# A state-space scan fed by differences of its inputs, in a 12-stage decoder on one core

## The chip, the core and the metric

One core of a Trainium2 chip runs the whole program. The metric is the device time of one launch, in microseconds (us). Engines: PE (TensorE, matmul) with its weight loads (PEld), DVE (VectorE), ACT (ScalarE), POOL (GpSimd), and SP, which here only issues DMAs.

## The reference, cut to the stage that changes

The decoder has four layers of three parts each, and a layer norm closes every part. The change touches one part, the attention slot of layer 2 (L2a in the code), a state-space scan. There are 8 sequences of 256 positions, width 128, with 16 states for each of the 128 channels.

```python
BC = x @ W_in + b_in
Bm, Cm = (BC[..., :N], BC[..., N:])
dt = jax.nn.softplus((x @ W_dt1 + b_dt1) @ W_dt2 + b_dt2)
dt = jnp.clip(dt, 1e-07, 1000000.0)
tmp = A * dt[..., None]
A_bar = jnp.exp(tmp)
B_barX = jnp.expm1(tmp) / tmp * dt[..., None] * Bm[:, :, None, :] * x[..., None]
...
_, h = jax.lax.associative_scan(combine, (A_bar, B_barX), axis=1)
return jnp.sum(h * Cm[:, :, None, :], axis=-1) + D * x
...
x = _layernorm(x + _L2_attn_ref(x, ...), axis=-1)
```

So h[s] = a[s] h[s-1] + (a[s] - 1) / A * B[s] x[s], where a is the decay exp(A dt).

## The kernel before

**Layout.** Channels lie on the partitions. A sequence b is worked off in four chunks t = 4b to 4b+3 of 4 states x 256 positions = 1024 columns, so the stage has 32 chunks. Each engine has its own list of instructions, written out by hand in a loop over t; the constants SCAN_X ... SCAN_DONE say in which iteration the once-per-sequence steps of sequence b come (`due(t, offset, 4)`). An engine works its list strictly in order and waits on semaphores.

**One chunk**, with the lines of the profile:
- ACT, `scan_scaled` (L2474): eight 128x128 products x * B into SBUF (both 128-position halves, four states). `decays` (L2514, L2515): four times exp(A dt) into `decay`, four times tanh(A dt / 2) into `gain`.
- PE, `scan_inputs` (L1809): eight transposes bring x * B, channels on partitions, into two PSUM banks (0 and 1, or 2 and 3).
- DVE, `feed` (L3375): (decay + 1) * PSUM. POOL, `scan_gains` (L855): that times tanh, which makes (a - 1) B x; it also clears the first decay of each state (L854).
- DVE, `scan` (L3383): the recurrence over the 1024 columns, both operands from SBUF. Then (L3387) the states times C, which PE has spread over the partitions in banks 4 and 5 (`spread_c`, L1895: four fp32 matmuls with a 16-row operand).
- PE, `summed` (L1911): eight matmuls with diagonal matrices 1/A add the states into bank 6; L1906 adds D * x.

In the trace each of these fp32 matmuls is two rows (it is worked in two halves), and a transpose is one row.

**Once per sequence**, all of it in bank 7: transpose of x (`scan_turn_x`, L1784; copied by ACT L2434), projections C and low rank (`scan_project`, L1789, L1790; ACT L2444, L2445), step size and B (`scan_step_sizes`, L1795, L1797; DVE `scan_sized` L3264, L3267), softplus as a series (ACT L2452, L2454, L2461; DVE `scan_series` L3274, L3277 and `scan_softplus` L3298, L3299), and at the end residual (L3392), statistics (L3398, L3401), root on POOL (L864, L865) and norm (L3407).

**Before and behind.** The gated part L1f runs ahead of the stage and already holds the first steps of sequences 0 and 1; the attention part L2x follows.

## Time and profile before

| | |
|---|---|
| median of 3 runs | 1743.04 us (1739.76 to 1743.62) |
| span of the profiled execution | 1740.7 us |
| scan stage, first scan to the last norm | 765.1 to 974.9 us |
| one sequence in the middle of the stage | 26.7 us |
| ACT busy in that sequence | 25.57 us |
| DVE busy in that sequence | 25.57 us |
| PE busy in that sequence, clock 1.00 | 22.72 us |

The profiled execution is known by its span, 1740.7 us; the median of the runs lies 2.3 us above it. Busy times are unions of an engine's rows, and those of PE hold the modelled tail of a matmul too. A clock of 1.00 is 2.4 GHz, 0.50 is 1.2 GHz.

### The profile page before, as it was taken

How to read it: one execution, taken by the hardware profiler on the slowest of the kernel's cores; microseconds unless marked ns; L12 is line 12 of the kernel's file. 1: busy time of each engine (PE TensorE's matmuls, PEld its weight loads, DVE VectorE, ACT ScalarE, POOL GpSimd, SP SyncE). 2: the span in 40 equal slices, each digit the busy share in tenths (PEclk: the TensorE clock that was granted, in tenths of full speed). 3: DMA queues.
4: the chain of work that ended last, by engine and by line, in shares of the span. 5: the costliest groups of instructions: out<-in, count | busy, mean ns of one | idle time of the engine just before them, and what ended most of it. 6: DMA issues, size and time to landing. Idle time of an engine off the chain costs nothing.

```text
span 1740.7 us, 34480 instructions
## 1 busy us (share of the span) xinstructions
PE 1516.1 (87%) x12731; PEld 1088.4 (63%) x12741; DVE 1273.2 (73%) x2817; ACT 1069.6 (61%) x2219; POOL 691.6 (40%) x801
## 2 busy tenths in 40 slices
PE   6588868799998898889989999998989998989875
PEld 5344436578777555667768766665548994655542
DVE  2688863697775798479999667758873448858988
ACT  4499942367665577399999155546763443157765
POOL 2455635578887022356767313320000101511223
PEclk9799979899999999989898989999998999999985
DMA  3200121200000000010000100000000000000000
GB/s 133 111 13 14 37 93 37 61 10 2 1 1 1 2 2 2 4 37 1 1 1 1 58 2 2 2 13 1 2 2 1 1 1 11 1 19 2 2 2 25
DMA packets 14791, 30.94 MB, mean 18 GB/s; under 512 B 1537, under 2 KB 10145, under 8 KB 13857
## 3 DMA queue, kind: packets, MB, share of 16 engines
q1 hardware_dynamic: 13602, 26.63, 4.4%
q0 software_dynamic: 1024, 2.10, 0.4%
q8 instruction: 104, 1.70, 0.4%
q14 instruction: 61, 0.50, 0.1%
HBM read 22.42 MB, written 6.29 MB: 16 GB/s over the span
## 4 chain that ended last, share of the span: by engine, by line
PE 44%; DVE 15%; ACT 14%; issue 12%; POOL 12%; DMA 1%; SPq 0%; POOLq 0%; DVEq 0%; ACTq 0%
PE PS L1412 5%; PE PS L1472 4%; ACT big L2261 4%; POOL big L837 4%; DVE negmax L2802 3%; PE PS L1744 3%; PE PS L1733 3%; POOL big L825 3%; ACT big L2239 2%; PE PS L1494 2%; POOL big L833 2%; PE PS L1417 2%; PE PS L1911 2%; PE PS L1895 2%; DVE V L3383 2%
## 5 line engine op out<-in xcount | busy, mean ns | idle before, releaser
L2239 ACT ACTIVATE big<-PS 128x1024 f32<-128x1024 f32 (+1 forms) x256 | 249.0, 974 | 163.4 <-PE PS L1423 162.7
L2802 DVE TENSOR_REDUCE negmax<-PS 128x4 f32<-128x1024 f32 x192 | 235.0, 1224 | 54.3 <-PE PS L1412 52.2
L1412 PE MATMUL PS<-KS,QS 32*128 32x256 f32 (+1 forms) x1152 | 133.2, 316 | 36.1 <-DVE negmax L2802 25.9
L1412 PEld LDWEIGHTS PS<-KS,QS 32*128 32x128 f32 x1152 | 86.7, 187 | 109.7 <-DVE negmax L2802 71.5
L711 POOL TENSOR_TENSOR rstd<-veps,mhalf 128x2 f32<-128x2 f32 x72 | 51.3, 712 | 242.2 <-DVE veps L2676 232.7
L1423 PE MATMUL PS<-QS,KS 32*128 32x256 f32 (+1 forms) x1152 | 133.7, 319 | 1.4 <-ACT big L2239 1.4
L1472 PE MATMUL PS<-big,V 128*32 128x256 f32 (+1 forms) x2048 | 133.0, 378 | 0.4 <-ACT big L2239 0.4
L737 POOL TENSOR_TENSOR res<-resb,XB 128x256 f32<-128x256 f32 x24 | 17.4, 727 | 258.5 <-ACT resb L2325 258.5
L779 POOL TENSOR_SCALAR KT<-QT 128x1024 f32<-128x1024 f32 x64 | 66.6, 1040 | 66.6 <-DVE QT L2821 62.7
L2821 DVE SCALAR_TENSOR_TENSOR QT<-PS,wint 128x1024 f32<-128x1024 f32 x64 | 77.3, 1220 | 17.9 <-PE PS L1365 17.2
L1423 PEld LDWEIGHTS PS<-QS,KS 32*128 32x128 f32 x1152 | 84.8, 188 | 5.8 <-issue 4.0
L2416 ACT ACTIVATE QT<-PS,W 128x256 f32<-128x256 f32 x128 | 53.6, 470 | 55.6 <-PE PS L1733 55.6
L825 POOL TENSOR_SCALAR big<-big,rsum 128x256 f32<-128x256 f32 (+1 forms) x144 | 60.7, 434 | 68.0 <-DVE rsum L2723 67.6
L1468 PE MATMUL PS<-big,V 128*32 128x512 f32 x512 | 64.5, 623 | 23.0 <-ACT big L2261 17.0
L837 POOL TENSOR_TENSOR big<-big 128x512 f32<-128x512 f32 x64 | 81.3, 1270 | 5.0
L1472 PEld LDWEIGHTS PS<-big,V 128*32 128x32 f32 x2048 | 54.1, 110 | 43.7 <-issue 14.3
L1129 PE MATMUL PS<-OT,W 128*128 128x256 f32 x272 | 75.5, 400 | 6.4 <-ACT QT L2187 6.4
L2187 ACT COPY QT<-PS 64x256 f32<-64x256 f32 x128 | 46.8, 366 | 53.0 <-DVE big L2707 51.3
L2261 ACT ACTIVATE big<-KT,W 128x1024 f32<-128x1024 f32 x64 | 73.0, 1141 | 9.0 <-POOL KT L779 9.0
L1895 PE MATMUL PS<-OT,SEL 16*128 16x256 f32 x256 | 67.5, 405 | 11.9 <-DVE V L3387 10.8
L1911 PE MATMUL PS<-On,V 128*128 128x128 f32 x512 | 77.2, 315 | 0.0
L1911 PEld LDWEIGHTS PS<-On,V 128*128 128x128 f32 x512 | 71.9, 225 | 7.9 <-issue 7.9
(479 smaller groups left out, 4323.8 us busy)
## 6 DMA issues: line engine op xcount, KB each, us to landing
W<-in_wpack SPq DMA_DIRECT2D x1, 4180.0 KB, 13.9
W<-in_wpack SPq DMA_DIRECT2D x1, 2560.0 KB, 9.0
W<-in_wpack SPq DMA_DIRECT2D x1, 2449.5 KB, 8.0
y_rows<-one_more SPq DMA_DIRECT2D x1, 2048.0 KB, 9.0
masks<-in_mask SPq DMA_DIRECT2D x8, 256.0 KB, 2.9
x_rows<-x_tok SPq DMA_DIRECT2D x16, 128.0 KB, 2.1
W<-in_wpack SPq DMA_DIRECT2D x1, 1538.0 KB, 5.9
x_tok<-in_x SPq DMA_DIRECT2D x1, 1024.0 KB, 4.8
```

Of the source, the lines that this page charges most:

```text
L825: ins = nc.gpsimd.tensor_scalar(PRW[:, u % 4, c0:c1], PRW[:, u % 4, c0:c1], rsum[:, u % 16, j:j + 1], 1.0, ALU.mult, ALU.mult)
L837: nc.gpsimd.tensor_tensor(q, q, RTW[:, u % 4, :, :], ALU.add).then_inc(sem("t_rope"), 1)
L1129: mm = nc.tensor.matmul(PS[:, QKB[u % 2], k * S:(k + 1) * S], w(f"{n}_w{x}", h * P, (h + 1) * P), OT[:, b, :], start=True, stop=True)
L1412: mm = nc.tensor.matmul(PS[:, MAXB[half], o], QS[r, bm % 2, tm, j * P:(j + 1) * P], KS[r, bm % 2, tm, k], start=not a.causal, stop=last)
L1423: mm = nc.tensor.matmul(PS[:, exp_banks(ge)[half], o], KS[r, be % 2, te, kb * P:(kb + 1) * P], QS[r, be % 2, te, q], start=not a.causal, s ...
L1472: mm = nc.tensor.matmul(out_rows[:, skip:S], v, PX[:, T % 2, h, kb * S:(kb + 1) * S - skip], start=first, stop=last)
L1895: mm = nc.tensor.matmul(PS[:, CB + k // 2, (k % 2) * S:(k % 2 + 1) * S], SEL[:, 4 * c + k, :], C_rows(b), start=True, stop=True)
L1911: mm = nc.tensor.matmul(PS[:, YB, j * P:(j + 1) * P], chunk("h", t)[:, at:at + P], by_state[:, 4 * c + k, :], start=False, stop=c == 3 and ...
L2239: nc.scalar.activation(PX[:, T % 2, 2 * p:2 * p + 2, 0:cols], PS[:, exp_banks(g)[0]:exp_banks(g)[0] + 2, 0:cols], ACT.Exp, scale=a.scale). ...
L2261: nc.scalar.activation((PX, PX2)[k][:, T % 2, 2 * p:2 * p + 2, :], clipped((QT, KT)[k], g), ACT.Exp, scale=a.scale, bias=w(("high_base", " ...
L2802: ins = nc.vector.tensor_reduce(negmax[:, h:h + 2, :].rearrange("p h j -> p (h j)"), banks.rearrange("p h (j k) -> p (h j) k", j=2), AX.X, ...
L2821: nc.vector.scalar_tensor_tensor(clipped(QT, g), PS[:, pair_banks(g):pair_banks(g) + 2, :], -100.0 / a.scale, capT[:, g // PAIRS % 2, :].u ...
```

## The change

The scan is summed by parts. Write v[s] = B[s] x[s] and leave the 1/A to the diagonal matrices, so that h[s] = a[s] h[s-1] + (a[s] - 1) v[s]. With g[s] = h[s] + v[s+1] this becomes g[s] = a[s] g[s-1] + (v[s+1] - v[s]): the scan's input is a difference of neighbours, and a - 1 is not needed. At the end x[s+1] times the sum over states of C[s] B[s+1] / A is taken off ("crossed"). In detail:
- ACT: `decays` makes only the exponentials (the tanh row is gone), in 255 columns each, since the first decays stay zero. `scan_scaled` makes four products instead of eight; POOL makes the other half in one instruction of 512 columns. New on ACT: `start` (copies the 4 first states into the PSUM chunk, once per chunk), the first decay and first inputs, one more projection copy, and `copy_result`. Two DVE jobs (bias and absolute value of the step size) go to ACT.
- PE: `scan_inputs` no longer transposes. It multiplies by a matrix of differences `L2a_ahead`, eight fp32 matmuls of 128 columns, and twice per chunk a matmul of 2 columns bridges the halves. `spread_c` uses the reduced fp32 type F32R on a 48-row operand that holds C as two parts. `summed` has the states as the moving operand, four matmuls of 256 columns. New per sequence: a projection of B, the matmul for the first inputs, `cross`, and `result`, two transposes back.
- DVE: `feed` is gone; the scan takes its second operand from PSUM. New per sequence: `scan_crossed_rows` (two instructions on 16 partitions), `crossed_inputs`, and `read_y` in place of the residual.
- POOL: `scan_gains` is gone; new are `scan_scaled`, `scan_signed`, `scan_first_state`.

```diff
-SCAN_X, ..., SCAN_DT, SCAN_Y, SCAN_DONE = -9, -8, -7, -6, -5, -4, -3, 5, 7
+SCAN_X, ..., SCAN_DT = -9, -8, -7, -6, -5, -4, -3
+SCAN_START, SCAN_CROSS, SCAN_Y, SCAN_OUT, SCAN_STATS, SCAN_DONE = -2, 2, 4, 6, 7, 8
...
-            def scan_gains(t):
-                pool.wait_ge(sem("L2a_fed"), t + 1)
...
-                nc.gpsimd.tensor_tensor(chunk("gain", t), chunk("gain", t), fed_to(t), ALU.mult).then_inc(sem("L2a_gain"), 1)
+            def scan_scaled(t):
...
+                if t >= 2:
+                    pool.wait_ge(sem("L2a_xB"), t - 1)
+                nc.gpsimd.tensor_tensor(chunk("x", t)[:, 512:1024].rearrange("p (k d) -> p k d", k=4),
...
+            def scan_first_state(b):
+                pool.wait_ge(sem("L2a_bc"), 2 * b + 3)
+                pool.wait_ge(sem("L2a_decay"), 5 * b + 1)
...
             def scan_inputs(t):
                 pe.wait_ge(sem("L2a_xs"), t + 1)
+                pe.wait_ge(sem("L2a_xs_second"), t + 1)
                 if t >= 2:
-                    pe.wait_ge(sem("L2a_fed"), t - 1)
-                for k in range(4):
-                    for j in range(2):
...
-                        mm = nc.tensor.transpose(PS[:, bank, (k % 2) * S + j * P:(k % 2) * S + (j + 1) * P],
-                                                 chunk("x", t)[:, at:at + P], ident)
+                    pe.wait_ge(sem("L2a_scan"), t - 1)
+                b, c = t // 4, t % 4
+                for h in range(2):
...
+                        nc.tensor.matmul(bank[:, first:first + P], chunk("x", t)[:, k * P:(k + 1) * P], w("L2a_ahead", 1),
+                                         start=k % 2 == 0, stop=False)
+                    nc.tensor.matmul(bank.rearrange("p (k c) -> p k c", k=2)[:, :, P - 1], x_tok[0:1, 2 * b + 1, :],
+                                     B_cols(b)[0:1, 16 + 4 * c + 2 * h:18 + 4 * c + 2 * h], start=False, stop=False)
...
+                def cross(b):
+                    bank_free(b)
+                    nc.tensor.matmul(PS[:, 7, 0:S], w(f"{n}_AT", rows=16), CB_rows(b), start=True, stop=True)\
...
+                def result(b):
+                    pe.wait_ge(sem(f"{n}_y_read"), 2 * b + 2)
...
                 for t in range(4 * B + 1):
-                    if t >= 4 and t + 2 < 4 * B:
-                        scan_inputs(t + 2)
+                    if 0 < t < 4 * B:
+                        spread_c(t)
+                    if t:
+                        summed(t - 1)
                     if (b := due(t, SCAN_PROJECT, 4)) is not None:
...
+                    if t + 2 < 4 * B:
+                        scan_inputs(t + 2)
+                result(B - 1)
...
                     for k in range(4):
-                        i, at = 4 * c + k, slice(k * S, (k + 1) * S)
-                        nc.scalar.activation(chunk("decay", t)[:, at], step_size(b), ACT.Exp, scale=w(f"{n}_A", i, i + 1))
-                        ins = nc.scalar.activation(chunk("gain", t)[:, at], step_size(b), ACT.Tanh, scale=negmax[:, i, 0:1])
+                        i = 4 * c + k
+                        ins = nc.scalar.activation(chunk("decay", t)[:, k * S + 1:(k + 1) * S], step_size(b)[:, 1:S], ACT.Exp,
+                                                   scale=w(f"{n}_A", i, i + 1))
...
+                def start(t):
+                    act.wait_ge(sem(f"{n}_xB"), t + 1)
...
+            def scan_crossed_rows(b):
+                dve.wait_ge(sem("L2a_bc"), 2 * b + 2)
...
-                def feed(t):
...
-                    dve.wait_ge(sem(f"{n}_gain"), t + 1)
+                    dve.wait_ge(sem(f"{n}_decay"), t + t // 4 + 2)
+                    dve.wait_ge(sem(f"{n}_started"), t + 1)
...
-                    nc.vector.tensor_tensor_scan(h, chunk("decay", t), chunk("gain", t), 0.0, ALU.mult, ALU.add)\
+                    nc.vector.tensor_tensor_scan(h, chunk("decay", t), flat(PS[:, bank:bank + 2, :]), 0.0, ALU.mult, ALU.add)\
```

The order of PE's instructions, from the matmuls with C of one chunk on. On PE before, one iteration with the projections and the next (OT holds C, On the diagonals, W and QT the transposes):

```order
L1895 MATMUL PS<-OT,SEL 128x256 x4
L1911 MATMUL PS<-On,V 128x128 x8
L1809 MATMUL PS<-W,QT 128x128 x8
L1789 MATMUL PS<-KT,W 16x256
L1790 MATMUL PS<-KT,W 64x256
L1895 MATMUL PS<-OT,SEL 128x256 x4
```

The same place of PE in the changed kernel, whose own line numbers these are (L1987 is the spread of C, L1999 the sum, L1895, L1897 and L1901 the differences of one half chunk, L1868 to L1870 the projections):

```order
L1987 MATMUL PS<-KS,SEL 128x256 x4
L1999 MATMUL PS<-V,On 128x256 x4
L1868 MATMUL PS<-KT,W 16x256
L1869 MATMUL PS<-KT,W 64x256
L1870 MATMUL PS<-KT,W 16x256
L1895 MATMUL PS<-W,QT 128x128 x2
L1897 MATMUL PS<-rt,x_tok 128x2
L1901 MATMUL PS<-W,QT 128x128 x2
L1895 MATMUL PS<-W,QT 128x128 x2
L1897 MATMUL PS<-rt,x_tok 128x2
L1901 MATMUL PS<-W,QT 128x128 x2
L1987 MATMUL PS<-KS,SEL 128x256 x4
```

The eight transposes have become ten matmuls, and they moved from ahead of the projections to the very end of the iteration, right in front of the next spread of C.

On DVE before, from the product with C of the chunk in which a step size falls due to the next one:

```order
L3387 TENSOR_TENSOR V<-V,PS 128x1024
L3277 SCALAR_TENSOR_TENSOR xs<-masks,xs 128x256 x2
L3392 TENSOR_TENSOR res<-PS,x_tok 128x256
L3298 SCALAR_TENSOR_TENSOR OT<-OT,xs 128x256
L3299 SCALAR_TENSOR_TENSOR KT<-OT,KT 128x256
L3375 SCALAR_TENSOR_TENSOR one_more<-big,PS 128x1024
L3383 SCALAR_TENSOR_TENSOR V<-big 128x1024
L3387 TENSOR_TENSOR V<-V,PS 128x1024
```

The same place of DVE in the changed kernel (L3542 is the product with C, L3554 `read_y`, L3412 and L3413 the crossed rows, L3433 the series, L3457 and L3458 the softplus, L3538 the scan):

```order
L3542 TENSOR_TENSOR V<-V,PS 128x1024
L3554 TENSOR_TENSOR XB<-PS,XB 128x256
L3412 TENSOR_TENSOR KS<-one_more,KS 16x256
L3413 SCALAR_TENSOR_TENSOR one_more<-PS,W,one_more 16x255
L3433 SCALAR_TENSOR_TENSOR xs<-masks,xs 128x256 x2
L3457 SCALAR_TENSOR_TENSOR OT<-OT,xs 128x256
L3458 SCALAR_TENSOR_TENSOR KT<-OT,KT 128x256
L3538 SCALAR_TENSOR_TENSOR V<-big,PS 128x1024
L3542 TENSOR_TENSOR V<-V,PS 128x1024
```

The 1024-column feed ahead of the scan is gone, and two 16-partition rows that wait for this sequence's projections stand between `read_y` and the series.

## Rows read from the trace of the kernel before

**Rows 1.** The page: span, busy time of each engine.
```profile
span 1740.7 us, 34480 instructions
PE 1516.1 (87%) x12731; PEld 1088.4 (63%) x12741; DVE 1273.2 (73%) x2817; ACT 1069.6 (61%) x2219; POOL 691.6 (40%) x801
```
**Rows 2.** Windows: start:end, length, busy us (rows) per engine, clock, DMA.
```profile
core 0: us, PE busy (x) PEld busy (x) DVE busy (x) ACT busy (x) POOL busy (x), PEclk, DMA share, GB/s
785.00:944.30 159.30, 146.46 (x861) 120.82 (x861) 151.85 (x165) 153.75 (x440) 108.91 (x61) 0.91 0.00 1
865.40:892.10 26.70, 22.72 (x145) 18.22 (x144) 25.57 (x28) 25.57 (x74) 18.09 (x10) 1.00 0.00 1
785.00:799.00 14.00, 14.00 (x89) 11.29 (x89) 12.97 (x12) 14.00 (x41) 9.41 (x5) 1.00 0.00 1
800.00:803.00 3.00, 3.00 (x15) 3.00 (x15) 3.00 (x3) 3.00 (x10) 1.70 (x2) 0.50 0.03 5
```
**Rows 3.** Groups of ACT by line, 865.4 to 892.1 us.
```profile
L2474 ACT ACTIVATE QT<-x_tok,rt 128x128 f32<-128x128 f32 x32 | 9.7, 386 | 0.0
L2515 ACT ACTIVATE big<-KT,negmax 128x256 f32<-128x256 f32 x16 | 7.9, 494 | 0.0
```
**Rows 4.** Groups of DVE by line, 865.4 to 892.1 us.
```profile
L3383 DVE TENSOR_TENSOR_SCAN V<-big 128x1024 f32<-128x1024 f32 x4 | 9.1, 2284 | 0.0
L3387 DVE TENSOR_TENSOR V<-V,PS 128x1024 f32<-128x1024 f32 x4 | 4.9, 1221 | 0.1
L3375 DVE SCALAR_TENSOR_TENSOR one_more<-big,PS 128x1024 f32<-128x1024 f32 x2 | 2.4, 1216 | 0.8 <-ACT big L2515 0.8
L3274 DVE SCALAR_TENSOR_TENSOR xs<-KT 128x256 f32<-128x256 f32 x1 | 1.3, 1283 | 0.0
L3267 DVE TENSOR_SCALAR OT<-PS,W 128x256 f32<-128x256 f32 x1 | 0.5, 474 | 0.0
```
**Rows 5.** Chain that ended last, pieces: start us, us to the next piece.
```profile
825.25 0.55 PE PS L1797 x4
834.27 1.92 PE PS L1895 x8
836.19 1.98 PE PS L1911 x16
838.17 0.87 PE PS L1809 x8
839.04 0.22 PE PS L1784 x2
844.03 0.54 PE PS L1789 x2
```
**Rows 6.** POOL's 512-column product elsewhere: ns min/median/max.
```profile
L837 POOL TENSOR_TENSOR big<-big x64: 1261/1269/1323, 333.9 to 551.2; 128x512 f32<-128x512 f32 x64
```
**Rows 7.** Timeline where the stage starts: start, us, idle before in brackets.
```profile
764.73 2.59 POOL L855 TENSOR_TENSOR big<-big,wint 128x1024 f32<-128x1024 f32 x1
765.14 4.33 DVE L3383 TENSOR_TENSOR_SCAN V<-big 128x1024 f32<-128x1024 f32 x1
770.77 1.35 PEld L1895 LDWEIGHTS PS<-OT,SEL 16*128 16x128 f32 x4 [3.49 <-DVE V L3387]
```
**Rows 8.** Timeline of DVE: products with C of chunks 3, 27 and 31.
```profile
789.28 1.22 DVE L3387 TENSOR_TENSOR V<-V,PS 128x1024 f32<-128x1024 f32 x1
...
948.43 1.22 DVE L3387 TENSOR_TENSOR V<-V,PS 128x1024 f32<-128x1024 f32 x1
...
968.01 1.22 DVE L3387 TENSOR_TENSOR V<-V,PS 128x1024 f32<-128x1024 f32 x1
```
**Rows 9.** Timeline where the stage ends.
```profile
971.85 0.69 PE L1264 MATMUL PS<-misc,W 32*128 32x256 f32 x2
971.96 0.42 DVE L3392 TENSOR_TENSOR res<-PS,x_tok 128x256 f32<-128x256 f32 x1 [2.72 <-PE PS L1911]
974.28 0.62 DVE L3407 SCALAR_TENSOR_TENSOR x_tok<-res,mv,rstd 128x128 f32<-128x128 f32 x2 [1.09 <-POOL rstd L865]
```

More of the change, by code:

```diff
@@ L27 @@
 CAPACITY = 256
-CONSTS, EARLY = 12, 6
+CONSTS, EARLY = 13, 6
 TERM = 8
@@ L521, in z_of, with first_inputs, first_decay, first_state @@
             return OT[:, 6 + b % 2, :]
-        low_rank, series = OT[0:64, 4, :], xs[:, :, :].rearrange("p j c -> p (j c)")
+        low_rank, series = OT[64:128, 4, :], xs[:, :, :].rearrange("p j c -> p (j c)")
+        crossed, summed_x = (XB[:, k, :, :].rearrange("p j d -> p (j d)") for k in range(2))
+        scan_zeros = big[:, 0:4096].rearrange("p (n c) -> p n c", c=S)[:, :, 0:1]
+        signed_B = sums[0:2, :, :].rearrange("p a b -> p (a b)")
+        def first_inputs(b):
+            return KT[:, 7, 136 + 32 * (b % 2):168 + 32 * (b % 2)]
+        def first_decay(b):
+            return KT[:, 7, 200:216]
+        def first_state(b):
+            return KT[:, 7, 216 + 16 * (b % 2):232 + 16 * (b % 2)]
+        def result_bank(b):
+            return 4 if b == B - 1 else 7
         def u_of(b):
@@ L2538, in L2a @@
                         decays(t + 2)
+                    if t + 1 < 4 * B:
+                        start(t + 1)
+                    if t == -1:
+                        scan_turned_x(2)
+                    elif t % 4 == 3 and 3 <= (t + 9) // 4 <= B:
+                        scan_turned_x((t + 9) // 4)
+                    if (b := due(t, SCAN_PROJECT, 4)) is not None:
+                        scan_projected(b)
+                    if (b := due(t, SCAN_STEP_SIZE, 4)) is not None:
+                        scan_small_exponential(b)
+                    if (b := due(t, SCAN_OUT, 4)) is not None:
+                        copy_result(b)
+                    if (b := due(t, SCAN_RATIO, 4)) is not None and b >= 2:
+                        scan_squares(b, 2)
+                    if (b := due(t, SCAN_U, 4)) is not None:
+                        scan_squares(b, 0)
             def L3a():
@@ L3429, in L2a @@
                         scan_series(b, 3, 5)
-                    if (b := due(t, SCAN_Y, 4)) is not None:
+                    if (b := due(t, SCAN_STATS, 4)) is not None and b < B - 1:
                         deviations(b)
+                deviations(B - 1)
+                norm(B - 1)
             def L3a():
```

305 lines of the change are left out of this document (204 added, 101 removed).

## The prediction

> **What bounds the kernel now.** I read the page first: in the whole program PE is busy 87% and DVE 73% [rows 1], an average over twelve stages that says little of one. The change lives in 210 us of it, so the windows of this stage come next. In one sequence in its middle, 26.7 us long, ACT and DVE are each busy 25.57 us and PE 22.72 us, at a clock of 1.00 [rows 2]. So two engines share the bound and PE has 4 us to spare. Over six sequences (785.0 to 944.3) it looks the same, with one difference: the mean clock of PE is 0.91 [rows 2]. A clock is 1.00 or 0.50, so PE spent 18% of 159.3 us, about 29 us, at half clock, and lost 14 us of work there, 2.4 us a sequence. That was free as long as ACT and DVE set the pace.
>
> The products with C give the rhythm: chunk 3 at 789.28, chunk 27 at 948.43, chunk 31 at 968.01 [rows 8]. Six sequences in 159.15 us make 26.5 us each. The start is worse than the middle: the first scan took 4.33 us, where the mean of later ones is 2.28, since POOL's L855 had started just before it; PE then stood idle for 3.49 us behind it [rows 4, 7].
>
> **The change, part by part, per sequence (four chunks).**
>
> ACT: sixteen tanh rows go. Sixteen rows cost 7.9 us, and as many exponentials stay. Of 32 scaling products (9.7 us) half go, 4.85 us [rows 3]. Added: four `start` copies, first decay, first inputs, one projection copy, two step-size rows in place of one, `copy_result`. The trace has no row of 4 or 16 columns on ACT; bounds are nothing and the 386 ns of a 128-column product [rows 3]. I take 0.35 us each, since small rows do not get much shorter, for nine rows 3.2 us. ACT: 25.57 - 7.9 - 4.85 + 3.2 = 16.0 us. It is no bound any more, even at 386 ns each.
>
> DVE: four feeds go, each 1.21 us, 4.8 in all, and the bias row of 0.47 [rows 4]. Added: two rows on 16 partitions and `crossed_inputs`, three rows like the 0.42 us of L3392 [rows 9], plus the step between two, 1.35 us. `read_y` replaces L3392 at its price. That gives 21.6 us. The scan now reads PSUM. That form is not in the trace; it lies between no change (the product L3387, also SBUF with PSUM, costs 1.22 us for 1024 columns, the feed of the same kind 1.22) and the 4.33 us of the slow first scan [rows 4, 7]. I take 2.3, by the two rows with a PSUM operand. POOL has less to do: its one 1024-column product (2.59 us and more [rows 7]) becomes a 512-column one, 1.27 us [rows 6]. DVE rows that stretch beside POOL now, such as the 1.28 us of L3274 at a width where L3392 takes 0.42, can shorten, by up to 2.5 us a sequence. So 19.1 to 21.6 us, and with two waits that the new order puts on DVE (the crossed rows stand behind ACT's three projection copies; the norm stands right behind the statistics and POOL's root, which took 1.09 us of waiting at the end [rows 9]) about 22.5.
>
> PE, from the pieces of the chain at full clock [rows 5]:
> - Spread of C: 8 rows of 0.24 us become 4 rows of one pass. A row of 128 columns of an fp32 matmul, which is half the matmul's work on half the columns, takes 0.124 (1.98 / 16); 256 columns in one pass I take at 0.12, at most 0.24. 4 x (0.48 - 1.92) = -5.8 us, at the dear end -3.8.
> - Differences in place of transposes: 8 rows, 0.87 us, become 16 rows of 0.124, 1.98 us: 4 x 1.11 = +4.4 us.
> - Two bridging matmuls of 2 columns per chunk are 4 rows; L1797 with 16 columns takes 0.55 / 4 = 0.137 each: +2.2 us. Below, 0.11 as for a transpose: +1.7.
> - Once: B's projection and `cross`, each like L1789, 0.54; the first inputs 0.27; `result` like L1784, 0.22: +1.6 us.
>
> Together +2.4 us (+4.4 with the dear spread). By pieces PE's work of before is 4 x (1.92 + 1.98 + 0.87) = 19.1 and some 3.0 for the rest, 22.1 us; the 22.72 busy hold tails of matmuls whose next one waited. After: 24.5 us. PE becomes the bound, against 26.5 for a sequence now.
>
> Does anything add to PE's own work? I walked one sequence with these durations. PE's iteration is spread, sum, extras, differences. The differences of chunk t+2 need the end of scan t (they overwrite its bank). The scan starts when the previous product with C is through, the product starts some 0.6 us after the iteration, and PE reaches the differences 2.4 us into it at the earliest, 4.1 with the projections. That fits in three iterations of four. In the one after the projections it is close: ACT copies them from about 4.1 us on, DVE does the crossed rows until 6.4, series and softplus until 8.2, the next scan until 10.5, while PE wants that scan's end at 10.6. One DVE row of the series that stands behind POOL's 1.27 us product costs PE up to 1.2 us. I add half of that, 0.6: 25.1 us a sequence. Queued behind PE's wait are the next spread and with it DVE's product, so what is lost there is lost for the stage.
>
> **PE's clock** decides whether 25.1 holds. The half-clock stretches of before lie in the stage's spread rows and waits (800 to 803: 15 rows in 3 us, clock 0.50, ahead of it 785 to 799 with no idle time and clock 1.00 [rows 2]). In the changed kernel the 16-row spread, 40% of PE's time in a chunk, shrinks to a tenth, full-height matmuls fill the rest, and the waits that PE has now (3.49 us at the start [rows 7]) mostly go. I take the clock as full in the middle of the stage. The trace also speaks against it, since 785 to 799 was dense and a fall came all the same. The Trainium skill (TensorE: Matmul & The Clock Gate, "What's actually happening") says that activity releases the throttle; by that alone a PE that never waits would stay at full clock, and the sum would be the one without falls. Rows 2 disagree with it in this form, so the falls keep a chance below.
>
> **The sum.**
> - Middle: 6 x (25.1 - 26.5) = -8.4 us.
> - Start: the first scan no longer waits behind feed and series (about 2 us), does not meet L855 (4.33 - 2.28 = 2.05 us), and PE does not wait 3.49 us for it and then work at half clock. These overlap; by the same walk chunk 3's product comes at 781 to 784 in place of 789.28: -5 to -8, taken as -6. The Trainium skill (SBUF — State Buffer, "Who interferes with whom") says that a DVE instruction with one SBUF input does not contend with GpSimd and one with two does; the 4.33 us row agrees, and it would give the 2.05 us in full.
> - End: from the last product (968.01) to the norm (974.28) come two transposes, an ACT copy and their handoffs, +1.3 us; L2x's first matmul (971.85 [rows 9]) stands behind them on PE, +1.2. The four last chunks, 19.6 us now, have no differences to make and stay as they are within 1 us.
> - Ahead, L1f: one 1024-column clear and half products on POOL, hidden in DVE's and POOL's waits there; nothing, at worst +1.
>
> -8.4 - 6 + 1.3 = -13.1 us against the profiled 1740.7, that is 1727.6; the median stands 2.3 above the span, so 1730 us.
>
> **Rivals.**
> - All handoffs hide and small rows are cheap: PE 24.0, start -8: 6 x -2.5 - 8 + 1.3 = -21.7, 1721 us. For it: ACT and POOL have much slack. Against it: the tight place above. Chance 0.17.
> - The half clock stays as it was: 2.4 us a sequence now fall on the bounding engine: 27.5 us. +6 - 4 + 1.3 = +3, 1740 to 1746 us. For it: falls in dense stretches. Against it: the spread of 16 rows shrinks. Chance 0.15, split over all three signs.
> - DVE's order becomes the bound (crossed rows waiting for ACT, the norm for POOL's root, series rows behind POOL): 26.3 us a sequence, -1.2 - 5 + 1.3, 1738 us. Chance 0.10.
> - Slower: the scan is dearer from PSUM. DVE has 22.5 us with its waits. Start and end give -4.7, so slower by 3.5 us needs 27.9 us a sequence, 1.35 us more per scan: it decides from 3.6 us a scan on. At the 4.33 us of rows 7, DVE needs 30.7, +25 - 4.7, 1763 us. Against it stand both rows with a PSUM operand at 1.22 us. Chance 0.08.
> - The forecast: PE bounds at nearly full clock, 24.6 to 25.7 us a sequence: 1724 to 1736. Chance 0.50.
>
> **Numbers.** A measurement here tells some 0.2%, 3.5 us, from no change: 1739.6 to 1746.5. Faster: 0.50 + 0.17 + 0.08 of the DVE case + 0.05 of the clock case = 0.80. Same: 0.02 + 0.06 + 0.01 = 0.09. Slower: 0.11 with 0.04 of the clock case and 0.07 of the scan. The range runs from just below the best case to the middle of the clock case, 1719 to 1743.
>
> **What the profile after would show.** The scan at 2.3 us with PS among its inputs; the spread at 0.5 us a chunk; differences 2.4 to 2.5 us; ACT near 16 busy us a sequence and DVE near 20; PE without gaps but before the differences that follow the projections; clock near 1.00 from chunk 3 on; 25 us from one fourth chunk to the next. I am wrong if the clock row stays at 0.91, if the scan grows, or if PE's rows show waits for DVE in more than one iteration of four.

## The result and the profile after

The changed kernel took 1757.44 us (median of 5) beside 1743.22 us for the kernel before (5 runs): a ratio of 1.0059, 95% interval 1.0034 to 1.0084. It is slower by about 0.6%, where 0.8% faster was forecast. One execution of the changed kernel took 2164.1 us at a mean clock of 0.635; it is in the median and left out of the ratio (the other four have a median of 1756.55 us). Ten further runs on another chip gave 1743.26 us beside 1740.08 us and a ratio of 1.0048 (1.0016 to 1.0081). So it is slower on both chips. The ratios on record are not quotients of the medians, and differ from them by up to 0.3% (1743.26 / 1740.08 is 1.0018, not 1.0048), so neither settles a difference of that size.

The page of the profiled execution, the rows that answer to [rows 1]:

```profile
span 1749.6 us, 34427 instructions
PE 1531.1 (88%) x12779; PEld 1092.2 (62%) x12789; DVE 1233.0 (70%) x2803; ACT 1000.2 (57%) x2035; POOL 600.7 (34%) x795
```

DVE lost 40 us of work, ACT 69 and POOL 91, and PE gained 15. The kernel got slower with less work on every engine but one. The windows of the stage, with the columns of [rows 2], first six sequences (from the product with C of chunk 3 to that of chunk 27), then one of them:

```profile
802.08:960.00 157.92, 157.92 (x887) 124.49 (x888) 118.74 (x147) 97.75 (x292) 34.41 (x52) 1.00 0.00 1
828.96:855.84 26.88, 26.88 (x151) 20.96 (x151) 20.27 (x27) 16.90 (x51) 5.97 (x10) 1.00 0.00 1
```

PE has no gap and is at full clock all the way: it is the bound. ACT (16.90) and DVE (20.27) are far from it. But a sequence takes 26.88 us, as long as before (26.77 from product to product).

The timeline of DVE (start, us, idle before), which answers to [rows 7, 8]: the first scan, and the products with C of chunks 3, 27 and 31.

```profile
782.07 2.29 DVE L3538 TENSOR_TENSOR_SCAN V<-big,PS 128x1024 f32<-128x1024 f32 x1 [2.39 <-ACT PS L2649]
...
802.08 1.22 DVE L3542 TENSOR_TENSOR V<-V,PS 128x1024 f32<-128x1024 f32 x1 [1.11 <-PE PS L1987]
...
960.00 1.22 DVE L3542 TENSOR_TENSOR V<-V,PS 128x1024 f32<-128x1024 f32 x1 [1.10 <-PE PS L1987]
...
981.92 1.22 DVE L3542 TENSOR_TENSOR V<-V,PS 128x1024 f32<-128x1024 f32 x1
```

The first scan is 17 us late (782.07 against 765.14). From it to chunk 3 it now takes 20.0 us, where it took 24.1. The first scan is released by ACT's copy, and two of the three products by PE's spread, where before PE's spread waited for DVE [rows 7]: who waits for whom has turned round.

The lateness has two parts. The first lies far ahead of the change. The timeline of PE, the first transpose of x for the scan, in the kernel before and in the changed kernel:

```profile
724.67 0.69 PE L1784 MATMUL PS<-W,x_tok 128*128 128x128 f32 x2 [6.12 <-POOL x_tok L988]
```
```profile
730.56 0.66 PE L1860 MATMUL PS<-W,x_tok 128*128 128x128 f32 x2 [6.22 <-POOL x_tok L1056]
```

Here 5.9 us are already gone. They went between 288 and 305 us: a DVE row that the change does not touch, and the window around it, in which the kernel before has 113 rows of PE at clock 1.00.

```profile
294.55 0.61 DVE L3314 TENSOR_SCALAR V<-PS,one_more 128x128 f32<-128x128 f32 x2 [5.40 <-remote]
...
288.00:305.00 17.00, 13.36 (x84) 11.76 (x83) 2.50 (x8) 4.71 (x12) 11.28 (x12) 0.90 0.16 47
```

The second part is L1f. From the first transpose to the first scan it was 40.5 us and is 51.5 us (782.07 - 730.56). PE's timeline in the changed kernel, at the two steps that make the step sizes of sequences 0 and 1:

```profile
742.32 0.67 PE L1878 MATMUL PS<-OT,W 64*128 64x256 f32 x2 [2.28 <-DVE one_more L3413]
...
743.38 2.34 PE L1925 MATMUL PS<-QT,big 128*128 128x256 f32 x6
...
747.75 1.46 PE L1925 MATMUL PS<-QT,big 128*128 128x256 f32 x6
...
764.27 1.01 PE L1878 MATMUL PS<-OT,W 64*128 64x256 f32 x2 [4.17 <-DVE one_more L3413]
...
766.09 2.91 PE L1925 MATMUL PS<-QT,big 128*128 128x256 f32 x6
```

PE waits 2.28 and 4.17 us for DVE's crossed rows (L3413), a wait that the change added. Behind each wait, a group of six widening rows takes 2.34 and 2.91 us, and at full clock 1.46. From the start of the step sizes to the next group at full clock it is 5.4 us (742.32 to 747.75) and 7.1 us (764.27 to 771.32), where the same rows took 3.8 us each time before; the granted clock of the two stretches was 0.69 and 0.52.

In the middle, the rows of PE for one chunk's differences, spread and sum:

```profile
828.12 0.73 PE L1987 MATMUL PS<-KS,SEL 48*128 48x256 f32 x4
828.78 1.99 PE L1999 MATMUL PS<-V,On 128*128 128x256 f32 x8
...
831.25 0.71 PE L1895 MATMUL PS<-W,QT 128*128 128x128 f32 x4
831.89 0.38 PE L1897 MATMUL PS<-rt,x_tok 1*128 1x2 f32 x2
832.20 0.71 PE L1901 MATMUL PS<-W,QT 128*128 128x128 f32 x4
832.75 0.61 PE L1895 MATMUL PS<-W,QT 128*128 128x128 f32 x4
833.29 0.38 PE L1897 MATMUL PS<-rt,x_tok 1*128 1x2 f32 x2
833.60 0.71 PE L1901 MATMUL PS<-W,QT 128*128 128x128 f32 x4
834.24 0.74 PE L1987 MATMUL PS<-KS,SEL 48*128 48x256 f32 x4
```

From start to start, the spread takes 0.66 us (forecast 0.48) and the differences 834.24 - 831.25 = 2.99 us (forecast 2.45). The two rows of one bridge start 0.31 us ahead of what follows them, near the 0.27 priced. But four full rows take 0.54 to 0.64 us next to a bridge, and without one 0.45 (shown below, at the kernel without bridges).

The groups of DVE and ACT in the same window, which answer to [rows 3, 4]:

```profile
L3538 DVE TENSOR_TENSOR_SCAN V<-big,PS 128x1024 f32<-128x1024 f32 x4 | 9.1, 2276 | 0.0
...
L3458 DVE SCALAR_TENSOR_TENSOR KT<-OT,KT 128x256 f32<-128x256 f32 x1 | 1.1, 1145 | 0.0
...
L3457 DVE SCALAR_TENSOR_TENSOR OT<-OT,xs 128x256 f32<-128x256 f32 x1 | 0.4, 424 | 0.0
```
```profile
L2649 ACT COPY PS<-KT 128x4 f32<-128x4 f32 x4 | 0.6, 150 | 0.0
```

### The profile page after: what moved, and what is told of

It reads as the page before. It is cut to its first block, busy times and chain, and to the rows that moved or that the text cites. A ratio compares the mean times of both kernels' runs of the same rounds, so it can differ in the third digit from the quotient of the medians.

```text
span 1749.6 us, 34427 instructions
## 1 busy us (share of the span) xinstructions
PE 1531.1 (88%) x12779; PEld 1092.2 (62%) x12789; DVE 1233.0 (70%) x2803; ACT 1000.2 (57%) x2035; POOL 600.7 (34%) x795
## 3 DMA queue, kind: packets, MB, share of 16 engines
q1 hardware_dynamic: 13602, 26.77, 4.5%
q0 software_dynamic: 1024, 2.10, 0.4%
## 4 chain that ended last, share of the span: by engine, by line
PE 51%; DVE 13%; POOL 12%; issue 12%; ACT 10%; DMA 1%; another core or an unknown queue 1%; SPq 0%; POOLq 0%; DVEq 0%; ACTq 0%
PE PS L1482 5%; PE PS L1542 4%; POOL big L869 4%; ACT big L2371 4%; DVE negmax L2950 3%; PE PS L1999 3%; PE PS L1814 3%; PE PS L1803 3%; POOL big L857 3%; PE PS L1901 2%; ACT big L2349 2%; PE PS L1564 2%; POOL big L865 2%; PE PS L1487 2%; PE PS L1895 2%
## 5 line engine op out<-in xcount | busy, mean ns | idle before, releaser
L743 POOL TENSOR_TENSOR rstd<-veps,mhalf 128x2 f32<-128x2 f32 x72 | 51.5, 715 | 250.4 <-DVE veps L2824 240.9
L3538 DVE TENSOR_TENSOR_SCAN V<-big,PS 128x1024 f32<-128x1024 f32 x32 | 72.9, 2278 | 3.6 <-ACT PS L2649 2.4
L2371 ACT ACTIVATE big<-QT,W 128x1024 f32<-128x1024 f32 x64 | 72.9, 1140 | 2.9 <-DVE QT L2969 2.8
L889 POOL TENSOR_TENSOR QT<-x_tok,rt 128x512 f32<-128x512 f32 x30 | 32.5, 1086 | 120.6 <-PE PS L1901 120.6
```

The lines of the kernel that those rows point to most:

```text
L2371: nc.scalar.activation((PX, PX2)[k][:, T % 2, 2 * p:2 * p + 2, :], clipped((QT, KT)[k], g), ACT.Exp, scale=a.scale, bias=w(("high_base", " ...
L3538: nc.vector.tensor_tensor_scan(h, chunk("decay", t), flat(PS[:, bank:bank + 2, :]), 0.0, ALU.mult, ALU.add)\
```

## The experiments

Ratios are to the kernel before, run on the same chip. "A sequence" is the time from one fourth chunk's product with C to the next in the profile. The first four kernels below shared a chip and 31 runs of the kernel before; the next four (the bridge on DVE to the spread on 16 rows) shared a second chip, the three after them a third, and the last had a fourth. Forecasts of medians in the first four are counted from the 1757 us of the first chip; on theirs the unedited changed kernel has 1743.26.

**The changed kernel once more.** 

> The changed kernel once more, unedited, for a second profile. In the first one 5.8 us of the 9 us that it lost on the kernel before were lost between 288 and 305 us, in a part that the change does not touch. Theory C, that stall is chance of one execution: it is gone or elsewhere in the second profile, the span is nearer to 1744, and the median stays near 1757 all the same if the median's runs have it elsewhere. Rival C2, it belongs to this program (its lists of instructions are longer): it stands at the same place, with the same length within 1 us.

Measured: ratio 1.0048 (1.0016 to 1.0081), median 1743.26 (10 runs), profiled span 1741.3. The window of 288 to 305 us, and the first transpose and first scan:

```profile
288.00:305.00 17.00, 15.92 (x111) 14.29 (x111) 3.71 (x11) 6.54 (x17) 13.03 (x14) 1.00 0.17 52
...
722.24 0.66 PE L1860 MATMUL PS<-W,x_tok 128*128 128x128 f32 x2 [6.22 <-POOL x_tok L1056]
...
773.79 2.29 DVE L3538 TENSOR_TENSOR_SCAN V<-big,PS 128x1024 f32<-128x1024 f32 x1 [2.39 <-ACT PS L2649]
```

The stall is gone (theory C): PE has 111 rows in the window in place of 84, at clock 1.00. The median did not stay near 1757, as the theory had added. What stalled in that one execution stays open. The first transpose comes 2.4 us earlier than before the change, so what lies ahead of it moves by several us from one execution to the next. The way from there to the first scan is 51.5 us again, and a sequence 26.9. This profile is the better one to read the change from.

**L1f in another order.**

```diff
 # DVE, L1f (what stood in the old places goes)
                     gated_residual(b - 1)
+                    if b in (3, 7):
+                        scan_crossed_rows(b // 7)
                     gated_product(b)
...
 # PE, L1f
-                    elif b in (3, 6):
-                        scan_step_sizes(b // 6)
+                    elif b in (3, 7):
+                        scan_step_sizes(b // 7)
```

> Edit: the changed kernel with another order in the gated part L1f only. DVE takes the crossed rows of sequences 0 and 1 before the gated product of sequence 3 and 7 (they stood after the product and the series), PE makes the step sizes of sequence 1 one iteration later (behind the second widening of sequence 7, not 6), and POOL's signs of sequence 1 follow. Theory A, PE waits in L1f for DVE's crossed rows (2.28 us at 742 and 4.17 us at 764) and then works at half clock: the first scan comes 5 to 9 us earlier, the stage is the same from there, median 1748 to 1752 (4 to 9 us under the changed kernel). Rival A2, L1f was late for another reason (constants on DVE, the projections themselves): the two waits move to another place and the median stays within 2 us of 1757.

Measured: ratio 1.0012 (0.9983 to 1.0041), median 1743.08. The medians of this kernel and the unedited one (1743.26) hardly differ, which is what rival A2 says of the median; the ratios do by 0.36%, with intervals that overlap, so the profile has to decide. PE's two waits and the first scan:

```profile
733.48 0.67 PE L1879 MATMUL PS<-OT,W 64*128 64x256 f32 x2 [1.05 <-DVE one_more L3414]
...
755.90 0.67 PE L1879 MATMUL PS<-OT,W 64*128 64x256 f32 x2 [2.19 <-DVE one_more L3414]
...
768.04 2.29 DVE L3540 TENSOR_TENSOR_SCAN V<-big,PS 128x1024 f32<-128x1024 f32 x1 [2.38 <-ACT PS L2650]
```

With a first transpose at 721.86 the way is 46.2 us, 5.3 less. The waits have halved, and the stage behind is unchanged (26.87 us a sequence). Theory A holds in the trace. The whole time does not show it: the stage ends 5.8 us earlier than in the second profile (974.55 against 980.36 us), but from there to the end it is 769.8 us in place of 760.9, in a part that the edit does not touch.

**Without the bridging matmuls.**

```diff
-                    nc.tensor.matmul(bank.rearrange(...)[:, :, P - 1], x_tok[0:1, 2 * b + 1, :],
-                                     B_cols(b)[0:1, ...], start=False, stop=False)
```

> Edit: the changed kernel without the two matmuls with a 1-row operand in each chunk that bridge the halves of 128 positions; the term of position 128 is left out of the scan's input. Theory B, what makes PE's sequence 26.9 us where 25.1 was predicted is the bridging: its own rows and a loss of 0.2 us at each change to an operand of one row; the differences of a chunk fall from 2.99 to 2.0 us, the sequence from 26.3 to 22.5 us, and over seven sequences 20 to 27 us go: median 1730 to 1737. Rival B2, the rows cost only their own time (0.14 us a row, 0.55 us a chunk) and the rest of the excess lies elsewhere: 24.3 us a sequence, median 1741 to 1744. Rival B3, DVE or the handoffs set the pace under PE: the sequence stays over 25 us.

Measured: ratio 0.9963 (0.9930 to 0.9996), median 1731.01, 12 us under the unedited kernel; 23.87 us a sequence. PE's timeline, one chunk's differences, and later the chunk that follows the step sizes:

```profile
865.32 0.71 PE L1895 MATMUL PS<-W,QT 128*128 128x128 f32 x4
865.87 0.61 PE L1899 MATMUL PS<-W,QT 128*128 128x128 f32 x4
866.32 0.61 PE L1895 MATMUL PS<-W,QT 128*128 128x128 f32 x4
866.76 0.61 PE L1899 MATMUL PS<-W,QT 128*128 128x128 f32 x4
867.30 0.74 PE L1985 MATMUL PS<-KS,SEL 48*128 48x256 f32 x4
...
878.69 0.68 PE L1895 MATMUL PS<-W,QT 128*128 128x128 f32 x4 [0.90 <-DVE V L3536]
```

The differences take 867.30 - 865.32 = 1.98 us, the 16 rows of 0.124 of the forecast. In detail two groups of four rows take 0.45 and 0.44, and the first and the last, each with something else at one side, 0.55 and 0.54. So the bridges cost 2.99 - 1.98 = 1.01 us a chunk, 4.0 a sequence, on PE. Only 3.0 of them show in the sequence, since a wait for the scan has come up: 0.90 us of idle time, and about 1.0 from start to start, since the matmul ahead of it shows its tail. Theory B has the price right, but not the 22.5 us a sequence (a mean over six; measured 23.7): the next bound is 1 us below.

**The two bridges side by side.** The bridges go behind the full matmuls of both banks, and from between them:

```diff
...
+                for h in range(2):
+                    bank = PS[:, (0, 2)[t % 2] + h, :]
+                    mm = nc.tensor.matmul(bank.rearrange(...)[:, :, P - 1], x_tok[0:1, ...], B_cols(b)[0:1, ...],
+                                          start=False, stop=True)
```

> Edit: the changed kernel with the two bridging matmuls of a chunk next to each other at the end of its differences, right ahead of the next spread of C, where each stood between full matmuls of its own bank. The work is the same. Theory B, a change between an operand of 128 rows and one of 1 row costs about 0.2 us on PE: two of four changes in a chunk go, 0.3 to 0.5 us a chunk, 1.2 to 2 us a sequence: median 1743 to 1749. Rival B2, the price is that of the rows themselves: no change, 1755 to 1759.

Measured: ratio 0.9979 (0.9945 to 1.0013), median 1735.13, 8 us under the unedited kernel; 25.45 us a sequence. PE's timeline:

```profile
869.89 0.71 PE L1895 MATMUL PS<-W,QT 128*128 128x128 f32 x4
...
871.87 0.60 PE L1903 MATMUL PS<-rt,x_tok 1*128 1x2 f32 x4
872.40 0.73 PE L1989 MATMUL PS<-KS,SEL 48*128 48x256 f32 x4
```

The differences take 2.51 us, 0.48 less, with the same rows in another order: 0.24 us for each of the two bridges that no longer stand between full matmuls. The 16 full rows take 1.98 again, where they took 2.37 with the bridges among them, and the four rows of the bridges 0.53 (872.40 - 871.87) in place of 0.62. A sequence falls by 1.43 us. That is 0.49 less than 4 x 0.48, because a gap has come up on PE here too. Theory B holds in its size. That the one row of the operand is the reason is not shown: no run has a bridge of 128 rows and 2 columns, and in the kernel without bridges a group of four full rows also takes 0.54 us behind the projection L1870 (871.55 to 872.09), whose operand has 128 rows.

**The bridge taken to DVE.** PE makes the 16 columns of a sequence once, beside the first inputs, ACT copies them, and DVE adds them:

```diff
+                    mm = nc.tensor.matmul(PS[:, 7, S + 32:S + 48], x_tok[0:1, 2 * (b - 1) + 1, :], B_cols(b - 1)[0:1, 16:32], ...)
...
+                    middle = PS[:, bank:bank + 2, :].rearrange(...)[:, :, :, P - 1]
+                    line.step(nc.vector.tensor_tensor(middle, middle, bridge(b)[:, 4 * c:4 * c + 4]..., ALU.add))
                     nc.vector.tensor_tensor_scan(
```

> Edit: the changed kernel with the bridging taken off PE's chunks. PE makes the 16 bridging columns of a sequence in one matmul (beside that of the first inputs), ACT copies them, and DVE adds four of them per chunk to the differences in PSUM ahead of the scan. Same computation. Theory B (two rows of the bridge and the two changes of operand height each cost PE, 1.0 us a chunk): PE's work falls by 4.0 us a sequence, less 0.5 for the new matmul; at the place where PE then waits for a scan, as without any bridge (0.90 us), it waits some 1 to 1.5 us, since DVE has one row more: 23.9 to 24.6 us a sequence, profile 13 to 18 us under that of the changed kernel, median 1727 to 1733. Rival D: the row of 4 columns with its step in front of each scan sits in the handoff that PE waits for in every chunk, and the sequence stays at 25.5 us or over, no better than the bridges side by side.

Measured: ratio 0.9989 (0.9966 to 1.0013), median 1734.71. Sequences: 24.27, 24.28, 24.44, 27.33, 25.84 us. Three are as theory B has them, and rival D, 25.5 us or over, is out. In the other two, half clock has come back (0.88 and 0.93), which neither theory had, and the median misses the 1727 to 1733 us expected. In the gain it stands no better than the bridges side by side.

**The bridge on DVE and a better order in L1f.**

```diff
 # DVE, L1f: crossed rows at once behind ACT's copies
+                    if b == 3:
+                        scan_crossed_rows(0)
                     gated_residual(b - 1)
+                    if b == 7:
+                        scan_sized(1)
...
                     elif b == 6:
+                        scan_crossed_rows(1)
                         scan_series(0, 3, 5)
 # PE, L1f: ahead of the second widening of sequence 7
+                    elif b == 7:
+                        scan_step_sizes(1)
 # POOL, L1f, b == 7, ahead of the root
+                        scan_first_state(0)
```

> Edit: the kernel with the bridging columns added by DVE, and with a new order in L1f: DVE takes the crossed rows of sequences 0 and 1 as soon as ACT has copied the projections, PE makes the step sizes of sequence 1 inside the iteration of the last sequence, and POOL makes the first state of sequence 0 ahead of its last root. Theory A (waits of PE in L1f, 1.05 and 2.19 us in the first new order, and 1.6 us of ACT for POOL's first state ahead of the first scan): from the first transpose of x to the first scan 42 to 44 us, where the changed kernel took 51.5 and the first new order 46.2. With the shorter sequence: median 1719 to 1725, 0.8 to 1.2% under the kernel before. Rival A2: the start is held by PE's work alone, and the new order is worth under 1 us more than the first: median 1723 to 1729.

Measured: ratio 0.9917 (0.9884 to 0.9949), median 1726.9. From the first transpose (722.39) to the first scan (765.47) it is 43.1 us, and PE no longer waits for the crossed rows at all: theory A, 8.4 of the 11 us of L1f are won back. Not all of the last step is PE's: this order also makes POOL's first state earlier, for which ACT stood idle 3.26 us ahead of its first copy in the changed kernel. The median is 2 us above the forecast; in the profiled execution the half clock in two sequences costs 6 us. The wait in the middle, the windows of a good sequence and a bad one, and then a longer wait in the sixth sequence, with its window:

```profile
825.38 0.68 PE L1901 MATMUL PS<-W,QT 128*128 128x128 f32 x4 [1.10 <-DVE V L3553]
...
809.47:833.73 24.26, 23.16 (x137) 18.30 (x136) 21.73 (x30) 16.86 (x52) 6.14 (x10) 1.00 0.00 1
...
858.17:885.50 27.33, 26.23 (x137) 20.54 (x137) 21.76 (x31) 16.83 (x52) 5.87 (x10) 0.88 0.00 1
...
921.29 0.68 PE L1901 MATMUL PS<-W,QT 128*128 128x128 f32 x4 [1.52 <-DVE V L3553]
...
913.00:936.15 23.15, 20.17 (x124) 16.81 (x123) 20.80 (x27) 13.34 (x43) 5.45 (x9) 1.00 0.01 1
```

**Side by side, with that order.** 

> Edit: the bridging matmuls side by side at the end of a chunk's differences, with the new order in L1f. If the two savings add: 25.45 us a sequence, first scan as early as with the other new order, median 1724 to 1730.

Measured: ratio 0.9938 (0.9917 to 0.9958), median 1726.55, 25.45 us in each of five sequences, 42.1 us to the first scan. As expected: the savings add. On the same chip this stands level with the bridge on DVE in that order (median 1726.9).

**The spread in fp32 again, on 16 rows.**

```diff
-    SEL[:, 4 * c + k, :], C_parts(b),
+    SEL[0:16, 4 * c + k, :].bitcast(F32), C_parts(b)[0:16, :].bitcast(F32),
```

> Edit: the changed kernel, but C is spread as before by fp32 matmuls with a 16-row operand, in two passes; the second part of C, which they do not take, is left out. Everything else stays. Theory E: PE sets the pace of the changed stage at full clock, so each of its microseconds counts: the spread goes from 0.66 back to 1.92 us, 5.0 us a sequence, about 35 us in the stage: 31.9 us a sequence and a median of 1776 to 1782. So without that part the rest of the change would lose 36 us. Rival E2: other handoffs set the pace and hide part of it: under 30.5 us a sequence.

Measured: ratio 1.0381 (1.0344 to 1.0419), median 1807.59, 35.2, 35.2, 33.6, 36.8 and 31.9 us in five sequences. The last is theory E's number to the tenth; the others are up to 5 us over it, and the median is 26 us over the 1776 to 1782 expected. Six sequences in one window:

```profile
799.81:1002.61 202.80, 202.80 (x983) 154.73 (x984) 119.75 (x148) 97.68 (x293) 34.28 (x51) 0.92 0.00 1
```

PE has no gap here, and yet a mean clock of 0.92. Between 840 and 950 us the half clock came six times, each time in the sum right behind a spread. This profile is that of the slowest of the four runs (1817.24 us).

**The same spread in fp32, on 48 rows.** As above, with all of `SEL` and `C_parts`. 

> Edit: the changed kernel with the spread of C in fp32, two passes, as in the run before with the fp32 spread, but on the 48-row operand (both parts of C; the computation is whole). With 16 rows PE had no gap, took 31.9 us in one sequence at clock 1.00 and 33.5 to 36.7 us in the others at 0.86 to 0.95. Theory G, the granted clock follows what the spread feeds to PE: with 48 rows the same gapless list keeps 1.00 and every sequence takes 31.9 to 32.2 us, median 1774 to 1780. Rival G2, the time in the spread decides, not its operand: the falls stay, 33 to 36 us a sequence, median 1795 or more.

Measured: ratio 1.0308 (1.0269 to 1.0346), median 1792.98, 31.88 us in each of five sequences.

```profile
797.36:985.31 187.95, 187.95 (x983) 145.61 (x984) 119.76 (x148) 97.76 (x293) 34.38 (x51) 1.00 0.00 1
```

The same 983 matmul rows in the same order, again without a gap, with each spread row as long at full clock (eight rows in 1.92 us). Only the height of the spread's operand differs, and the clock is 1.00. That is theory G in the profile, with one execution of each kernel, on two chips. The median is 13 us over the 1774 to 1780 expected. In the profiled execution 13 us are lost behind the stage: from its last norm to the end it is 774.1 us, and 760.9 in the changed kernel. With ratios 1.0381 and 1.0308, whose intervals touch, the two kernels differ by 0.7%, 12.7 us; their windows of six sequences differ by 202.80 - 187.95 = 14.9.

**DVE's step size behind the scan.** On the kernel with the bridge on DVE and the order in L1f:

```diff
-                    if b := due(t, SCAN_DT, 4):
-                        scan_softplus(b)
                     if 0 <= t < 4 * B:
                         scan(t)
+                    if b := due(t, SCAN_DT, 4):
+                        scan_softplus(b)
```

> Edit: the kernel with the bridging columns on DVE and the last order in L1f, with one more move: DVE makes a sequence's step size (two rows, 0.9 us) behind the scan and the product with C of its iteration, where they stood ahead of them. ACT needs the step size 2 us later than it then comes. Theory F: the 1.10 us that PE waits for a scan once in a sequence is the price of those two rows standing ahead of it, and the half clock that came back in two of the sequences (27.3 us in place of 24.3) follows such waits. The wait shrinks to 0.2 us or less, 23.2 to 23.5 us a sequence, clock 1.00 in all of them, median 1712 to 1718. Rival F2: the wait goes but the half clock comes in dense stretches too: two sequences stay over 26 us, median 1719 to 1723.

Measured: ratio 0.9872 (0.9835 to 0.9909), median 1718.12 against 1737.86. This is the fastest kernel of the study, 1.3% under the kernel before by the ratio and 1.1% by the medians. PE's wait, and six sequences:

```profile
821.15 0.68 PE L1901 MATMUL PS<-W,QT 128*128 128x128 f32 x4 [0.24 <-DVE V L3553]
...
783.23:926.33 143.10, 138.34 (x800) 109.99 (x800) 126.20 (x172) 96.47 (x295) 34.69 (x51) 0.98 0.00 1
```

The wait fell from 1.10 to 0.24 us and five sequences took 23.1 to 24.1 us at clock 1.00; a second wait of 0.27 to 0.63 us, for the scan before, has come up in four of them, which 23.2 to 23.5 had not counted. The sixth had half clock (0.53 from 911 to 917 us), behind a wait of 2.14 us for a scan at 909.94. Theory F holds for the wait that it named, and not for the clock in all six.

**The same move with the bridges side by side.** 

> Edit: the kernel with the bridging matmuls side by side and the last order in L1f, with DVE's step size behind the scan and the product. Here PE had no gap in the stage. Theory F: nothing to win, 25.45 us a sequence as before, median within 2 us of 1726.5. Rival F3: the order on DVE also costs PE something that no gap shows: 0.3 us a sequence or more go.

Measured: ratio 0.9938 (0.9918 to 0.9958), median 1726.54, but 24.96 us a sequence in place of 25.45. The expectation's premise was wrong, as two windows show, the one without the move and the one with it:

```profile
786.09:811.54 25.45, 25.10 (x151) 20.17 (x152) 19.10 (x21) 16.91 (x51) 5.08 (x8) 1.00 0.00 1
```
```profile
783.14:808.10 24.96, 24.96 (x151) 20.07 (x152) 18.29 (x21) 16.90 (x51) 5.08 (x8) 1.00 0.00 1
```

There had been a gap of 0.35 us, which the move closed; so rival F3 has the number, though the gap did show. With it closed, a sequence is 26.88 - 4 x 0.48 = 24.96 us, all that the bridges side by side save. The 2.5 us that this won in five sequences do not reach the median; what differs behind the stage is larger (below).

**One part of the change alone, in the kernel before:** the spread in one pass.

```diff
-        SEL = sb("SEL", [16, 16, P])
+        SEL = sb("SEL", [16, 16, P], F32R)
...
-            return OT[0:16, b % 4, :]
+            return KS[0:16, 0, b % 4, :]
```

> Edit: the kernel before, with one part of the change alone: C is spread in one pass in the reduced fp32 type, on a 16-row operand (what the rounding of C takes off is left out). Theory H: before, ACT and DVE set the pace of a sequence (25.57 us busy each of 26.7), so the 5 us that PE saves are worth nothing in the middle: 26.7 us a sequence, and only the start, where PE worked its spread behind a wait of 3.49 us, gives 0 to 2 us: median within 0.2% of the kernel before. Rival H2: PE's half clock and its order cost DVE more than busy times show; the sequence falls by 0.5 us or more and the median by 4 us or more.

Measured: ratio 1.0006 (0.9971 to 1.0040). A sequence is 26.77 us in both. The window that answers to the second row of [rows 2]:

```profile
865.40:892.10 26.70, 20.60 (x126) 18.07 (x126) 25.52 (x29) 25.57 (x74) 18.05 (x11) 0.83 0.00 1
```

ACT is busy 25.57 us as before; PE has more waits, a lower clock, and it costs nothing. From the first scan to chunk 3 it is 23.2 us in place of 24.1. Theory H holds.

## Why the prediction was wrong

**The account.** Between the kernel before and the second profile of the changed one: first transpose to first scan +11.1 us (51.5 against 40.5, rounded), first scan to chunk 3 -4.1 (20.0 against 24.1), chunk 3 to chunk 27 -1.2 (157.9 against 159.15), chunk 27 to 31 +2.3 (21.9 against 19.6), chunk 31 to the norm +0.5: 8.5 us. The forecast had 0, -6, -8.4, 0, +1.3. The two spans differ by 0.6 us alone, since the second profile had gained 2.4 us ahead of the stage and gained 5.5 behind it (760.9 us from the last norm to the end, before 766.4), 4 of them in L2x.

**The step that failed most** is "Ahead, L1f: one 1024-column clear and half products on POOL, hidden in DVE's and POOL's waits there; nothing, at worst +1". It measured +11. I priced what L1f had to do and not what it had to wait for. The diff showed the new wait: `scan_step_sizes` waits for DVE's crossed rows, since it overwrites the bank that they read. On DVE these stood behind the gated product and its copy, in the second case behind series and softplus too. PE works in order, so 6.5 us of waiting went into the way to the first scan, and the slow stretches behind the waits, 5.4 + 7.1 us in place of 2 x 3.8, account for the rest. In the middle of the stage I had asked of each wait what is queued behind it; in L1f I had not. Three orders show it: 51.5, 46.2 and 43.1 us, the last with POOL's first state moved as well.

**The second step** is the sum of PE, 24.5 us and 25.1 with the handoff, where 26.88 was measured. The mechanism was right: PE became the bound, at full clock, without a gap. A term was mis-sized: "Two bridging matmuls of 2 columns per chunk are 4 rows [...] +2.2 us". Measured, they cost 1.01 us a chunk, 4.0 a sequence: 0.53 us a chunk side by side, 2.1 a sequence, and 0.48 more, 1.9 a sequence, because each stands between full matmuls. The price came from L1797, four rows in a run with a 128-row operand, where nothing of the kind can be seen. The spread was 0.66 us in place of 0.48, +0.7 a sequence. The 0.6 us for the handoff did not arise, because PE was longer than forecast; without the bridges it stood there with 0.90 us, at the place where it was expected. So the middle gave -1.2 and not -8.4. DVE and ACT had been relieved by 5.3 and 8.7 us for it.

**What held.** The scan from PSUM takes 2.28 us (forecast 2.3), so the rival of a dearer scan is out. ACT has 16.9 us (16.0), DVE 20.3 (19.1 to 21.6). A copy of 4 columns on ACT is 0.150 us, not 0.35. The differences without bridges are 1.98 us as worked out, from rows of 0.11 and two ends of 0.09 that the forecast had not told apart. The start gave 4.1 of 6 us. The four last chunks were forecast as unchanged within 1 us and took 2.3 more.

**The clock.** It is full in the middle as forecast: 1.00 against 0.91. The reason given, that the 16-row spread shrinks in time, is not what the fp32 runs point to: with a spread as long as before the clock is 0.92 without a gap on a 16-row operand and 1.00 on 48 rows. So the height goes with the full clock, in one profile of each; the short spread on 16 rows was not run in the changed kernel, and being right here was in part luck. By the Trainium skill (TensorE: Matmul & The Clock Gate, "What's actually happening"), activity releases the throttle; a PE without gaps does not keep it released here, by the 0.92. Between chunk 3 and chunk 27 half clock came back behind two of the five waits of 1.10 us in the kernel with the bridge on DVE and the new order, behind two of five without that order, and behind the one of 2.14 us in the fastest kernel. There it did not behind the others, nor behind waits of 1.25 to 1.54 us in the sixth sequence of the two kernels with 1.10 and of the one without bridges, nor behind those of 0.90 or of 0.19 to 0.63 us. So a wait alone does not decide it, and what does stays open.

**What the change did not do.** The 5.9 us lost ahead of L1f in the first profile were not there in the second. And the 4 us that come back in L2x cannot be booked to the change: a stretch at half clock some 30 us behind the stage, at the same place of the program, stands in the kernel before, the one with its spread in one pass, the two with the fp32 spread, the one with the bridge on DVE, the fastest, and the side-by-side kernel with the moved step size (first row below); it is short in the one with L1f in another order, and missing in both profiles of the changed kernel and in four edits of it, among them the side-by-side kernel without the move (second row).

```profile
985.90:997.90 12.00, 12.00 (x88) 8.18 (x85) 5.67 (x14) 4.79 (x8) 1.41 (x2) 0.57 0.01 1
```
```profile
992.30:1004.30 12.00, 11.42 (x131) 7.87 (x128) 8.94 (x23) 6.67 (x11) 2.13 (x3) 1.00 0.01 1
```

Only the changed kernel has two profiles, so whether this belongs to the execution or to the program is not shown, and what sets it off was not tried. From the last norm to the end, in code that no edit touches, the profiles range from 757.9 us (side by side, without the move) to 773.9 (with it), and to 780.1 in the kernel with the fp32 spread on 16 rows. That is more than the moved step size won in the stage, and there the 2.5 us of that run may have gone. An edit worth a few microseconds must be read from the stage's own rows.

**Open.** Why the first chip saw a larger difference of medians (14 us) than the second (3 us), at ratios whose intervals overlap. And in the fastest kernel DVE still waits 3.19 us ahead of the first scan for ACT, which works through exponentials and scaling products; the start may have more to give.

## What to carry to other kernels

When a change moves an engine from slack to bound, every new wait on that engine must be walked through wherever it stands, also in the stage ahead, where the first steps run in advance: ask what must be finished, and behind what that is queued. Price a small matmul among large ones in its surroundings, not from a run of its like; here standing between full matmuls cost nearly as much again. Where the clock stayed full it was cheaper still to make its columns once per sequence and add them on an engine with slack (24.3 against 25.45 us a sequence), but the medians showed that only with the step size moved too. And try an order before giving up a change: the same result went from 0.5% slower to 1.3% faster by moving rows and one small sum.

## What the hardware showed unexpectedly

- A bridge, an fp32 matmul of 2 columns with a 1-row operand, costs PE 0.50 us between matmuls of 128 rows (2.99 against 1.98 us a chunk with two of them), and two side by side at the end of a chunk 0.53 together (2.51). Whether the height or the smallness does it was not separated.
- Operand height and clock: 983 gapless matmul rows, 0.92 with a 16-row spread, 1.00 with a 48-row one (one profile each).
- A DVE row of 256 columns with two SBUF inputs took 1.145 us where it met POOL's product (L3458; its like 0.42), while the scan, with one input in SBUF and one in PSUM, kept its 2.28 us beside it (scan from 833.88, POOL's product 834.39 to 835.43). The Trainium skill (SBUF — State Buffer, "Who interferes with whom") says that one SBUF input does not contend with GpSimd and two do; the trace agrees. L3457, with two SBUF inputs as well, started 0.02 us before POOL's product (841.67 and 841.69) and kept its 0.42 us, and the product took 1.31 us in place of 1.04.
